# Two-layer decoder on one core: SiLU as one ScalarE function in place of tanh and a vector operation, and the batch loops written out

## The reference, cut to what matters

```python
def _L0_ffn_ref(hidden_states, gate_w, gate_up_proj, down_proj):
    probs = jax.nn.softmax(x @ gate_w.T, axis=-1)
    w, idx = jax.lax.top_k(probs, TOP_K)                 # TOP_K = 2
    w = w / jnp.sum(w, axis=-1, keepdims=True)
    combine = jnp.zeros((T, E), x.dtype).at[jnp.arange(T)[:, None], idx].add(w)
    def step(acc, inputs):
        gup, dn, ce = inputs
        g, u = jnp.split(x @ gup.T, 2, axis=-1)
        acc = acc + ce[:, None] * (jax.nn.silu(g) * u @ dn.T)
...
x = _layernorm(x + _L0_attn_ref(...))    # attention over 7 neighbours: softmax
x = _layernorm(x + _L0_xattn_ref(...))   # additive attention: tanh over 512 x 77 x 128, softmax, gates
x = _layernorm(x + _L0_ffn_ref(...))     # the block above
x = _layernorm(x + _L1_attn_ref(...))    # top-32 attention, no exponential
x = _layernorm(x + _L1_xattn_ref(...))   # cross attention: softmax over 77 keys
x = _layernorm(x + _L1_ffn_ref(...))     # shared expert and 8 routed experts, exact GELU
```

## Time and profile before

| | us |
|---|---|
| median of 3 runs (892.77 to 893.54) | 893.12 |
| the profiled execution | 892.3 |
| its span in the trace | 889.9 |
| PE busy | 747.6 |
| DVE busy | 587.2 |
| ACT busy | 385.8 |
| POOL busy | 76.5 |

### The profile page before, as it was taken

The page is one execution under the profiler, slowest core; times in us unless marked ns, Lnnn a source line. Parts: engine busy times, 40 slices in busy tenths (PEclk is TensorE's granted clock), DMA queues, the critical chain, the costliest instruction groups (busy, mean ns, idle before and its releaser), DMA issues.

```text
span 889.9 us, 12254 instructions
## 1 busy us (share of the span) xinstructions
PE 747.6 (84%) x4056; PEld 516.2 (58%) x4056; DVE 587.2 (66%) x1548; ACT 385.8 (43%) x634; POOL 76.5 (9%) x71
## 2 busy tenths in 40 slices
PE   3468678989988988999988979899988999973596
PEld 1221156876245966776246857775347878852586
DVE  3568467885765677775755787864946687749344
ACT  1058632237875432237875432257864322211142
POOL 2100020110011120100011120100011000000100
PEclk8769979999998999999999999999998999987578
DMA  6025000000000010000000010000000000000000
GB/s 239 0 71 201 1 27 1 1 1 1 1 3 1 1 42 1 1 1 1 1 3 1 2 41 1 1 1 1 1 3 1 1 13 1 1 1 0 1 1 12
DMA packets 6558, 15.13 MB, mean 17 GB/s; under 512 B 2776, under 2 KB 2912, under 8 KB 6240
## 3 DMA queue, kind: packets, MB, share of 16 engines
q1 hardware_dynamic: 6496, 14.32, 4.8%
HBM read 13.27 MB, written 1.05 MB: 16 GB/s over the span
## 4 chain that ended last, share of the span: by engine, by line
issue 66%; PE 14%; DVE 10%; POOL 7%; ACT 1%; DMA 1%; SPq 1%; POOLq 0%; DVEq 0%; ACTq 0%
PE bank L643 3%; PE bank L602 2%; PE bank L504 1%; POOL b_rstd L1407 1%; PE bank L505 1%; PE bank L506 1%; POOL a_big L1417 1%; DVE a_big L1382 1%; DVE top L1265 1%; POOL b_y L1433 1%; DVE b_big L1269 1%; DVE gup_lo L1362 1%; POOL a_sum L1420 1%; POOL a_rstd L1403 1%; DMA rb_sb<-rb 1%
## 5 line engine op out<-in xcount | busy, mean ns | idle before, releaser
L878 ACT ACTIVATE b_big<-bank 128x512 f32<-128x512 f32 x128 | 75.7, 596 | 207.2 <-PE bank L506 207.1
L847 ACT ACTIVATE a_big<-a_sum,txt_cols 128x512 f32<-128x512 f32 x231 | 145.5, 712 | 14.2 <-PE bank L602 14.1
L602 PE MATMUL bank<-a_big,score_pad 128*32 128x512 f32 x616 | 143.9, 616 | 7.4 <-ACT a_big L967 5.8
L1227 DVE SCALAR_TENSOR_TENSOR b_big<-b_big,bank 128x512 f32<-128x512 f32 x128 | 87.3, 682 | 63.9 <-ACT b_big L878 59.9
L643 PEld LDWEIGHTS bank<-down_sb,b_big 128*128 128x128 f32 x1024 | 118.2, 192 | 6.1 <-issue 3.5
L504 PE MATMUL bank<-x_hi,gup_hi 128*128 128x512 f32 x256 | 112.4, 439 | 9.5 <-DVE b_big L1227 5.9
L643 PE MATMUL bank<-down_sb,b_big 128*128 128x128 f32 x1024 | 119.9, 276 | 0.0
L505 PE MATMUL bank<-x_hi,gup_lo 128*128 128x512 f32 x256 | 103.6, 405 | 0.0
L506 PE MATMUL bank<-x_lo,gup_hi 128*128 128x512 f32 x256 | 103.5, 404 | 0.0
L1233 DVE TENSOR_TENSOR b_big<-bank,b_big 128x512 f32<-128x512 f32 x128 | 88.5, 692 | 4.4
L602 PEld LDWEIGHTS bank<-a_big,score_pad 128*32 128x32 f32 x616 | 28.3, 109 | 101.2 <-ACT a_big L847 54.7
(11 more groups left out here) (215 smaller groups left out, 960.7 us busy)
## 6 DMA issues: line engine op xcount, KB each, us to landing
b_big<-gup SPq DMA_DIRECT2D x8, 512.0 KB, 6.5
down_sb<-down SPq DMA_DIRECT2D x1, 2048.0 KB, 8.2
rw_sb<-rw SPq DMA_DIRECT2D x1, 1152.0 KB, 10.4
a_T<-x_T SPq DMA_DIRECT2D x4, 256.0 KB, 2.6
a_tok<-x_tok SPq DMA_DIRECT2D x4, 256.0 KB, 3.1
b_big<-rw SPq DMA_DIRECT2D x2, 512.0 KB, 3.6
y<-b_tok SPq DMA_DIRECT2D x4, 256.0 KB, 2.0
const_sb<-const SPq DMA_DIRECT2D x1, 872.0 KB
```

The lines of the kernel that those rows point to most:

```text
L602: last = mm(P[2][32 * j:32 * j + 32, :], score_pad[:, 31 - i:63 - i], ring[k % RING], start=(i == 0), stop=(KCOL * (i + 1) + j >= KEYS))
L847: act(ring[k % RING], a_sum[:, 0:S], ACT.Tanh, bias=txt_cols[:, c:c + 1])\
L878: act(th[n % 3], P[3 + 2 * (c % 2)][:, :], ACT.Tanh, scale=0.5).then_inc(th_ready, 1)
L1227: stt(th[n % 3], th[n % 3], 1.0, P[3 + 2 * (c % 2)][:, :], ALU.add, ALU.mult)\
```

## The change

The tanh becomes the engine's SiLU function on g itself, the vector operation of line 1227 and its semaphore go, the gate bank is free when ACT has read it, the factor 0.5 leaves the routing weights (the operation stays, with two operands), and the five `Fori` loops become Python loops, so that all four passes are straight code with constant waits.

```diff
-            with eng.Fori(0, B - 2) as b:                      # SP
+            for b in range(B - 2):
...
-   for half, bank, freed, ready in ((0, P[3 + 2 * (c % 2)], t1_done, g_psum),      # PE, swiglu
+   for half, bank, freed, ready in ((0, P[3 + 2 * (c % 2)], th_ready, g_psum),
                                     (1, P[4 + 2 * (c % 2)], hid_ready, u_psum)):
...
-            with eng.Fori(0, B - 1) as b:                      # PE, ACT, DVE and POOL alike
+            for b in range(B - 1):
                 second_half(b, True)
             second_half(B - 1, False)
...
-                        act(th[n % 3], P[3 + 2 * (c % 2)][:, :], ACT.Tanh, scale=0.5).then_inc(th_ready, 1)
+                        act(th[n % 3], P[3 + 2 * (c % 2)][:, :], ACT.Silu).then_inc(th_ready, 1)
...
-                stt(r0_we, r0_we, 0.5, r_den[:, :].unsqueeze(2).broadcast_to(r_wide), ALU.mult, ALU.mult)\
-                    .then_inc(r_weights, 1)
+                tt(r0_we, r0_we, r_den[:, :].unsqueeze(2).broadcast_to(r_wide), ALU.mult).then_inc(r_weights, 1)
...
                         eng.wait_ge(th_ready, E * C0 * b + n + 1)
-                        stt(th[n % 3], th[n % 3], 1.0, P[3 + 2 * (c % 2)][:, :], ALU.add, ALU.mult)\
-                            .then_inc(t1_done, 1)
-                        eng.wait_ge(t1_done, E * C0 * b + n + 1)
                         eng.wait_ge(u_psum, E * C0 * b + n + 1)
```

More of the change, by code:

```diff
@@ L381, in decoder @@
         th_ready = sem("th_ready")
-        t1_done = sem("t1_done")
         hid_ready = sem("hid_ready")
@@ L970, in _ @@
             turned_x2(0)
-            with eng.Fori(0, B - 1) as b:
+            for b in range(B - 1):
                 second_half(b, True)
```

## The result

| | before | after |
|---|---|---|
| median (us) | 893.33 (892.77 to 895.09) | 872.29 (870.16 to 873.84) |
| the profiled execution | 892.3 | 871.73 |
| its span | 889.9 | 869.9 |
| PE / DVE / ACT busy | 747.6 / 587.2 / 385.8 | 736.0 / 505.5 / 410.6 |

The ratio is 0.976, with an interval of 0.9734 to 0.9785: 21 us faster, where 13 were forecast. Applied to the 893.12 us on which the forecast stands, the ratio gives 871.7, just under 872, the low end of the wider range.

The account below looks back on a forecast made before the run. PE bounds swiglu, with DVE second, so DVE savings count only where PE waits for DVE. Terms 11.0 + 2.7 + 0.7 + 1.8 + 2.4 - 3.6 - 1.9 = 13.1 us gave 880.0 us; range 875 to 885, eight in ten 872 to 890.

Parts of the forecast that it names:

- the price of the vector operation: Removing line 1227's DVE operation: 16.2 us won, from head sums 11.0, gate bank 2.7, batch 3 0.7, output product 1.8.
- Head sums, 11.0: PE's three waits ahead of line 553 shrink, 6.8 us, and the slow matmuls behind them go, 4.2 us.
- Gate bank, 2.7: ACT's read frees the bank one DVE operation earlier; eight gate product waits for line 1227 go, 2.7 us won.
- rival 4: DVE was the true pace in more places than the waits name; upper bounds, 22 us won, 871 us; chance 0.08.
- Output product, 1.8: PE's three waits ahead of line 583 each shrink near 0.6 us by one removed DVE operation: 1.8 us won.
- GELU, not in the sum: The table load ahead of GELU was already there, so no gain or loss was forecast for this stretch.
- Batch 3, 0.7: At step 2 the wait moves from gate to up product, winning only three matmuls: 0.7 us, bounds 0 to 2.1.
- The turns, 2.4: With loops written out, input DMAs land 2.97 us after issue instead of 4.16; 1.2 us won at each of two turns.
- Step 10, 3.6: Two table loads around the exponential make PE wait at step 13's gate product, 1.2 us in three passes: 3.6 lost.
- Cross attention, 1.9: A table load ahead of its exponential delays it 0.63 us, which PE waits for: 1.9 us lost in three passes.
- The tables: On ACT, SiLU's table serves tanh but not the exponential: 27 table loads, against 9 before.
- a drain of 1.38 us: If each table switch on ACT also paid the skill page's drain, the gain would be 0.7 us; chance 0.03.

Follow-up runs that it names:

- sum of four steps: Successive run differences: loops written out -8.4 us, gate bank freed with the operation replaced +6.4, that operation gone -27.6, SiLU's table loads +8.1; all -21.4.
- best version: Kernel after, with step 10's exponential moved to step 9 and a one-element exponential at the head of the cross attention: 863.46 us, ratio 0.9664.

## Why the prediction was wrong, point by point

The step that failed is the price of the vector operation: I took it from the waits that named it or its followers, 16.2 us, and it came to 21.2 in the sum of four steps above. In that sum the gate bank's 2.7 stands for a mechanism that the runs do not show. The other mis-sized term is that of the loops, 2.4, which measured 8.4 alone and 4.1 in the changed kernel.

- **Head sums, 11.0: right, with some luck in the size.** 11.2 by the table. The waits fell from 7.4 to 1.1 us, a rest of 0.4 per wait where I left 0.2, and the slow matmuls went from 2.78 to 1.60: together 9.8 over three passes, and the rest is of other waits and spells in that stretch.
- **Gate bank, 2.7: the mechanism failed.** The up bank is held by hid, which ends 0.73 us after `t1`, and PE wants it 0.70 later, so where both hold, freeing the gate bank early only moves the wait. I had worked out just this for batch 3 ("the up product waits for hid of step 0") and not for the other eight waits. They went in the kernel after, where DVE was no longer late. This was rival 4: DVE the true pace in more places than the waits name.
- **Output product, 1.8: too high as a wait, too low as a stretch.** PE's wait fell from 5.3 to 4.3, by 1.0. But with no new loads the stretch from the head sums to the output product is 107.3 us over three passes against 111.3, and the one from there to the top attention 134.3 against 137.1: together 6.8 where gate bank and output product had 4.5.
- **GELU, not in the sum.** Without new loads this stretch is 98.6 us against 101.4; the kernel after has 101.7. From the router's first product to the end of PE's wait for the GELU it is 6.95, 6.46 and 6.95 us before and 5.83 to 5.84 after, with a mean clock of 0.55, 0.74 and 0.56 before and 1.00, 0.99 and 0.71 after. Before, the slow spell fell on the small products that start the chain to the GELU (line 511 takes 1.09 us before, 0.64 after); with DVE's operation gone it comes later or not at all. In the kernel after, a spell behind the wait takes the 2.8 us back (last section). Both profiles of after have it (101.7 and 103.3 us); the kernels without the two loads in line at step 10 take 98.6 to 100.6. So up to 3.1 us of what the loads cost lie here, where I had put none.
- **Batch 3, 0.7: too low.** 3.2 us with the first profile of after and 1.6 with the second: the wait goes from 2.98 to 2.09, now at the up product as forecast, and the slow spell behind it is gone in the first and there in the second. My upper bound was 2.1.
- **The turns, 2.4: mechanism right, size small.** The work behind the last DMA starts 2.96 and 3.30 us after its issue, forecast 2.97 for both. But SP also issues its last DMA 0.42 us sooner, 3.74 against 4.16 after PE's logits product, so the first turn gives 1.6 and the second 2.0, 3.6 together. Alone, the loops give 7 to 10; what the surplus is stays open.
- **Step 10, 3.6: right in kind, too low.** 1.7 a pass and not 1.2, 5.2 in all. The wait at step 13 is 1.03, close to the 1.1. I stopped there; the hid and the down product behind it are late as well (PE waits 0.16 to 0.2 for `b_y` in each pass, where it did not before).
- **Cross attention, 1.9: right,** 1.7 by the table, 0.57 to 0.6 in a pass.
- **The tables: right.** 27 loads, tanh shared, exponential not. The load of 1.28 us agrees with the Trainium skill, "ScalarE: Activation LUTs", section "What ACT_TABLE_LOAD costs". That section adds a drain of 1.38 us to each switch, by which, as the prediction estimated, 0.7 of the 13.1 us would have been left. No run here shows it: where ACT does not wait for data, the activation starts 0.01 to 0.02 us behind the load's end. The Trainium skill, same page, section "Table sets: the hidden batching unit", advises to do the calls of one table together. The switches cost about 8 us here, and moving two calls to where ACT idles took this cost away with as many loads as before the move.

So the sum missed by 8 us: 5 too little for the vector operation with the bank's release (21.2 where I had 16.2), 6 too little for the loops as they stand alone, and 3 too little cost for the loads. That the error is not larger is luck in part, since the last has the other sign. The chance of rival 4, 0.08, was too small: that PE's waits named L1227 nine times and L1233 not at all was no evidence that hid was in time. A wait shows only the first of two that end close together.

## What to carry to other kernels

When two banks of a step are freed by two operations of one engine in a row, and the consumer wants them in the same rhythm, the last one sets the pace: freeing the first early moved the wait here and showed no gain, while less work on that engine gained at such places, and at some that no wait names. When an operation is put back as a test, its own duration has to be looked at first: one that reads other memories can take another time beside another engine. Before counting a table load as a cost, look for idle time ahead of the call: a load runs ahead of the wait of its activation, so a call moved by one step, or an exponential of one element in front of a wait, can hide it, as both did here. And a stall of TensorE should be priced with the matmuls behind it, with a bound on either side, because the same stall cost 1.6 us more in one execution than in another.

## What the runs showed of the hardware that I had not expected

**Whether a slow spell of PE's clock cost anything depended on which side of a wait it lay.** In the kernel after and in the best version the wait for the GELU ends 5.84 us after the router's first product. In the kernel after, PE runs at full clock, waits 2.14 and is slow behind the wait:

```profile
463.45 1.06 PE L733 MATMUL bank<-router_sb,b_T 128*128 128x8 f32 x8 [0.69 <-ACT b_T L863]
...
469.29 0.80 PE L503 MATMUL bank<-b_hi,rw_hi 128*128 128x512 f32 x1 [2.14 <-ACT b_big L939]
469.88 0.63 PE L504 MATMUL bank<-b_hi,rw_lo 128*128 128x512 f32 x1
```

In the best version it is slow first, waits 0.60, and has its full clock behind:

```profile
459.21 1.06 PE L734 MATMUL bank<-router_sb,b_T 128*128 128x8 f32 x8 [0.69 <-ACT b_T L864]
...
465.05 0.51 PE L504 MATMUL bank<-b_hi,rw_hi 128*128 128x512 f32 x1 [0.60 <-ACT b_big L941]
465.39 0.40 PE L505 MATMUL bank<-b_hi,rw_lo 128*128 128x512 f32 x1
```

Ahead of the wait the spell costs nothing here, as it falls behind the small products that feed the chain; behind the wait it costs 1.5 us in this pair: the whole stretch takes 34.41 us in the first kernel and 32.87 in the second. PE's granted clock, the column behind its busy time, is 1.00 ahead of the wait and 0.50 behind it in the kernel after; these are the levels 2.4 and 1.2 GHz:

```profile
464.80:467.00 2.20, 2.20 (x11) 1.00 0.00 0
469.30:471.60 2.30, 2.30 (x8) 0.50 0.00 0
```

**The same wait is followed by a slow spell in one execution and not in the next.** In the two profiles of the loops alone, the same code on two chips, PE waits 2.79 and 2.78 us at the same matmul of batch 3. From each timeline, that matmul and one three further on, first of the one, then of the other:

```profile
708.91 0.50 PE L504 MATMUL bank<-x_hi,gup_hi 128*128 128x512 f32 x1 [2.79 <-DVE b_big L1227]
...
709.72 0.41 PE L504 MATMUL bank<-x_hi,gup_hi 128*128 128x512 f32 x1
```

```profile
711.63 0.50 PE L504 MATMUL bank<-x_hi,gup_hi 128*128 128x512 f32 x1 [2.78 <-DVE b_big L1227]
...
712.62 0.63 PE L504 MATMUL bank<-x_hi,gup_hi 128*128 128x512 f32 x1
```

The matmuls last 0.40 in the first; in the second eight last about 0.63, until 715.6, and the stretch of batch 3 takes 83.62 and 85.22 us. What decides it no run here shows.
